# Expert stage of a graph and mixture-of-experts layer: second layer and results three tiles behind the first layer instead of two

## What is computed

```python
x = x + gnn(layernorm(x), edges, W, b)        # agg[dst] = x[src]; [x, agg] @ W.T + b
t = layernorm(x)
p = softmax(t @ router_w.T); rw, re = top_k(p, 2); rw = rw / rw.sum()
out = t
for e in range(8):
    h = gelu(t @ w1[e] + b1[e])               # 256 -> 256
    out = out + combine[:, e] * (h @ w2[e] + b2[e])
x = x + out
```

## Time and profile before

| | |
|---|---|
| timed runs | 1039.62 us (1039.11 to 1040.34) |
| span of the profiled execution | 1216.1 us; no other time of it is given |
| PE, DVE, ACT, POOL busy over the span | 77%, 67%, 47%, 38% |
| expert stage in the span | about 748 to 1211 us |
| L928 | 3000 matmuls |
| L943 and L938 | 1500 and 250 matmuls |
| granted TensorE clock over the span | 0.868 of full |

### The profile page before, as it was taken

One profiled execution on the slowest core, in us unless ns is written; L12 is line 12 of the kernel. 1 busy time (PEld: TensorE's weight loads), 2 busy tenths in 40 slices (PEclk: granted clock), 3 DMA queues, 4 the chain that ended last, 5 costly groups with the idle time before them and its releaser, 6 DMA issues.

```text
span 1216.1 us, 28747 instructions
## 1 busy us (share of the span) xinstructions
PE 932.3 (77%) x9598; PEld 821.3 (68%) x9599; DVE 820.3 (67%) x1801; ACT 569.5 (47%) x1565; POOL 467.2 (38%) x529
## 2 busy tenths in 40 slices
PE   0488888888377888247659945999888889999987
PEld 0477777777266677137648924888677778878876
DVE  6999999998255555534637594776565666667656
ACT  1355555554144444034435523555454555555544
POOL 8000000001544445555455002555555555555553
PEclk9799999999698889655555557999999999999999
DMA  6920000001344433335345361222222222222220
GB/s 202 323 100 26 26 26 26 26 17 43 99 129 132 126 112 112 87 107 170 116 135 168 105 7 36 63 73 71 58 62 58 62 64 71 74 70 71 70 58 13
DMA packets 78990, 103.26 MB, mean 85 GB/s; under 512 B 22505, under 2 KB 64482, under 8 KB 78938
## 3 DMA queue, kind: packets, MB, share of 16 engines
q0 software_dynamic: 21408, 54.87, 16.0%
q1 hardware_dynamic: 57530, 47.73, 13.9%
HBM read 62.12 MB, written 44.02 MB: 87 GB/s over the span
## 4 chain that ended last, share of the span: by engine, by line
PE 43%; DVE 21%; another core or an unknown queue 13%; issue 12%; ACT 8%; ACTq 1%; DMA 1%; DVEq 0%; POOL 0%; POOLq 0%
PE bank L928 10%; PE bank L943 9%; DVE arena L1040 7%; PE bank L748 5%; DVE arena L1027 5%; PE bank L771 5%; PE bank L829 4%; PE bank L894 3%; PE bank L840 2%; ACT arena L720 2%; PE bank L938 2%; ACT arena L682 1%; PE bank L792 1%; ACT arena L589 1%
## 5 line engine op out<-in xcount | busy, mean ns | idle before, releaser
L492 POOL DMA_INDIRECT arena<-key_rows,cid x98 | 93.9, 959 | 370.7 <-DVEq L1135 272.3
L928 PE MATMUL bank<-arena,w1s 128*128 128x128 f16 x3000 | 199.6, 221 | 28.9 <-issue 24.8
L928 PEld LDWEIGHTS bank<-arena,w1s 128*128 x3000 | 180.2, 99 | 43.2 <-issue 39.1
L943 PE MATMUL bank<-w2s,arena 128*128 x1500 | 199.8, 274 | 0.9 <-issue 0.8
L519 POOL DMA_INDIRECT out<-arena,gidx x125 | 128.8, 1030 | 177.7 <-DVE arena L1338 114.2
L508 POOL DMA_INDIRECT arena<-tok_rows,gidx x125 | 125.3, 1002 | 107.6 <-DVE gidx L1314 69.7
L771 PE MATMUL bank<-wgs,arena 128*128 128x256 f16 x1176 | 162.7, 295 | 0.0
L943 PEld LDWEIGHTS bank<-w2s,arena 128*128 128x128 f16 x1500 | 147.6, 98 | 18.0 <-issue 0.9
L707 ACT ACTIVATE arena<-bank 128x256 f16<-128x256 f32 x125 | 48.1, 385 | 222.9 <-remote 139.4
L771 PEld LDWEIGHTS bank<-wgs,arena 128*128 128x128 f16 x1176 | 124.4, 106 | 27.6
L720 ACT ACTIVATE arena<-bank,b1s 128x128 f32<-128x128 f32 x500 | 142.1, 374 | 1.2 <-PE bank L928 1.2
(11 more groups left out here) (215 smaller groups left out, 1515.0 us busy)
## 6 DMA issues: line engine op xcount, KB each, us to landing
agg_rows<-arena SPq DMA_DIRECT2D x49, 256.0 KB
tok_rows<-arena SPq DMA_DIRECT2D x13, 896.0 KB
big<-x SPq DMA_DIRECT2D x6, 1792.0 KB, 15.1
arena<-w SPq DMA_DIRECT2D x16, 256.0 KB, 2.9
arena<-tok_rows,gidx POOLq DMA_INDIRECT x125
out<-arena,gidx POOLq DMA_INDIRECT x125
big<-x SPq DMA_DIRECT2D x1, 1664.0 KB
arena<-key_rows,cid POOLq DMA_INDIRECT x98
```

The source lines that it names most:

```text
L492: gp.indirect_dma_start(er[:, b % 2, s, :], None, key_rows, bass.IndirectOffsetOnAxis(cid[:, t:t + 1], 0)).then_inc(er_full[b % 2], 16)
L928: last = mm(bank[2 + u % 2][:, at:at + P], parts[x, w, c, f], a[:, u % 4, c * P:(c + 1) * P], start=(n == 0), stop=(n == 5))
L943: last = mm(to, a[:, u % 4, at:at + P], parts[x, w, c], start=False, stop=(n == 5))
```

## The change

PE's second layer and DVE's result are taken three tiles behind the first layer instead of two, and the last written-out steps are one more. The place of each in its engine's step stays as it was, and so do all the other distances (tokens two ahead, hidden layer one behind), the buffers and POOL's order.

```diff
+BEHIND = 3
@@ schedule
-            for j in range(last * DEPTH, NT + 2):
+            for j in range(last * DEPTH, NT + BEHIND):
@@ pe_step
-                if j is None or 0 <= j - 2 < NT:
-                    tile_out(*tile(i, u, -2), second_layer(experts_of(known, (u if j is None else j) - 2)))
+                if j is None or 0 <= j - BEHIND < NT:
+                    tile_out(*tile(i, u, -BEHIND), second_layer(experts_of(known, (u if j is None else j) - BEHIND)))
@@ dve_step
-                if j is None or 0 <= j - 2 < NT:
-                    result(*tile(i, u, -2))
+                if j is None or 0 <= j - BEHIND < NT:
+                    result(*tile(i, u, -BEHIND))
```

## The result

The changed kernel takes 1049.57 us (median of four runs, 1048.62 to 1050.37) where the kernel before takes 1039.36 beside it: a ratio of 1.0092, with an interval of 1.0076 to 1.0108. It is slower by about 10 us, and the prediction of 1039.5 with its range up to 1048 missed it. The execution profiled has a time of its own of 1050.37 us over a span of 1048.3.

A forecast was written before the change was run, and what follows sets the result against it. PE's own work was taken to bound the expert stage, 3.10 us a step, 388 of its 463 us. The terms 0 + 0 + 0 - 0.1 = -0.1 us took 1039.62 to 1039.5 us, with a range of 1030 to 1048.

The forecast's parts named there:

- The late signal: ACT's L707 starts 1.73 us late behind PE's transposes in dense stretches of the trace; taken as absent from timed runs.
- Part (a): PE's order, second layer one step later: worth between 0 and 11.6 us of waits for L1325, taken as 0.
- Part (b): DVE's order and the hidden layer's buffers, results taken one tile later: zero, covered by the extra step.
- Part (d): Both ends of the expert stage: from -0.3 to +0.2 us, taken as -0.1.
- Part (c): POOL's store and gather issues move one step back, the change's only price: 0, with the gather's slack falling from 3.8 us.
- the slack of 0.7 us: Gather with a prompt signal: rows there at H + 9.96, wanted at H + 10.64, H being the first-layer burst's start.
- The gather becomes late: Rival: gathered rows land after PE's transposes want them, holding PE up; 1047 us, bounds 1043 and 1059, chance 0.21.
- 2 x 1.0 less 1.6: Late-gather price per trip of eight: about 1.0 us added twice, some 1.6 of L1325 waits gone; given as 27.7 from 27.45.
- no change: Likeliest case: no change that can be told, part sum -0.1 us, own range 1038 to 1041, chance 0.52.
- The low half did hold PE up: Rival: PE's second layer loses 5.6 to 11.6 us waiting for DVE's L1325, which the change frees; 1031.5 us, chance 0.27.
- a matmul record's hidden tail: PE's matmul records: their end is only an estimate and semaphore passing lies outside, so waits for L1325 could be in timed runs.
- waits of L894 for the gather's DMA: Sign in the changed kernel's trace: PE's transposes should now and then wait for gathered rows.
- The last sign: Timed runs moving by over 2 us either way would make the prediction wrong, with the late signal in them.

The follow-up runs named there:

- e1: The kernel before, unchanged, run and profiled again: 1040.42 us.
- e5 to e8: On a chip where the kernel before took 1215.23 us: gather ahead of store at two and four behind, sixteen slots at three and two behind; 1263.19, 1254.92, 1233.1, 1226.99 us.
- e11: The changed kernel with 16 slots for gathered rows instead of 8: 1037.34 us, ratio 0.9970.
- e13: The changed kernel with 16 slots for gathered rows and second layer and results four tiles behind: 1036.6 us, ratio 0.9969.
- e2: The changed kernel with POOL issuing the gather ahead of the store: 1041.07 us, ratio 1.0016.
- e3: The kernel before, distance still two, with only the gather issued one step later: 1050.01 us, ratio 1.0096.
- e14: The changed kernel with second layer and results four tiles behind, 8 slots, and the gather issued ahead of the store: 1093.33 us, ratio 1.0512.
- e4: The changed kernel with second layer and results four tiles behind instead of three, nothing else: 1214.04 us, ratio 1.1689.
- e12: The kernel before with 16 slots for gathered rows instead of 8: 1042.28 us, ratio 1.0021.
- e10: The kernel before with PE's transposes also waiting for the first expert's output added to an earlier tile (L1335): 1069.2 us, ratio 1.0274.

## Why the prediction was wrong

**The readings that held.** The late signal was taken to be in no ordinary timed run, and it is in none (e1), though it is a condition of some chip and not of the recording (e5 to e8). Part (a) was put at 0, on the ground that with a prompt signal the second layer has 1.2 us to spare: e1 has a single wait of 0.2 us for L1325, and with it gone the kernel gained nothing. Part (b), DVE's order and the buffers, costs little or nothing: e11 and e13 run at three and four behind without a loss. e2's 0.16% over the kernel before sits at the ends of the trips, whose last step is longer by 0.66 us instead of 0.53 (14 x 0.13 = 1.8); why, was not followed up. Part (d) was within half a us of nothing, too small to be seen beside the rest. Part (c) named the gather's later issue as the only price of the change, and it is (e3 has all of it, e2 almost none).

**The step that failed** is the sum of part (c), the slack of 0.7 us. Its first terms hold: the result ends 4.91 us behind the burst's start (4.90 in the sum), the gather starts at 7.08 (7.06), and half of the gathers land within 2.8 us. Two terms were mis-sized. The first is the end of the sum, the time at which the rows are wanted. It was put at 1.34, the start of the transposes. PE's sequencer comes to them at 0.43 to 0.47 and stops if the rows are not there, and the second layer is late when it gets past them after 1.09 or, in three steps of eight, after 0.67. Three steps on, less the gather's start, that leaves a gather 9.27 + 1.09 - 7.08 = 3.28 us, or 2.86, where the sum had 10.64 - 7.06 = 3.58.

The second is the landing time, one value for all. 2.90 and 2.85 were the first two gathers of the stage; over the changed kernel's stage the median is 2.8, but one in five takes more than 3.3 us, one in ten more than 3.6, and the longest 4.0 (4.8 in e1). The two together are the loss, and neither alone: a gather of the median 2.8 us is in time in every step, and had rows been wanted only when the array wants them, the spread would have cost little: the transposes themselves are late in nine of 116 tiles, 2.6 us in all. The sequencer stops in 66 tiles. Most of these lose nothing; in 23 the second layer is late by more than 0.05 us, 8.3 us in sum, and that is the loss of the stage to within 1.2 us. In the kernel before, with one step more, even a gather of 4.8 us is in time.

The rows of the kernel before at hand could have shown the first term: the register instructions of PE's sequencer are in the trace with their times. I read PE's and the weight loads' rows alone and took the row of the array for the time at which a semaphore is needed.

The dose follows the same sum. A result is finished in the step that is `distance` behind its tile's, and the rows gathered behind it are wanted six steps after the tile's own, so that the slack is (6 - distance) x 3.09 + w - 2.9, less the gather's start in its step (for the late gather of e3, one step fewer). With w = 0.45 it is the slack until the sequencer stops; with the mean of the two limits over a trip (0.99 for two behind, 0.93 for three, 0.88 for four, where four steps are of the second kind) it is the slack until the second layer is late:

| | gather starts | slack to a stop, us | slack to a loss, us | measured loss, us |
|---|---|---|---|---|
| two behind (before) | 7.13 | +2.8 | +3.3 | 0 |
| three, gather first (e2) | 5.18 | +1.6 | +2.1 | 1 to 2 |
| three (after), two with a late gather (e3) | 7.08, 7.11 | -0.3 | +0.2 | 10 |
| four, gather first (e14) | 5.23 | -1.5 | -1.1 | 53 |
| four (e4) | 7.1 | -3.4 | -2.9 | 174 |
| three or four, sixteen slots (e11, e13) | 7.7 | over 20 | over 20 | -3 |

Where the slack to a loss is negative, the ring of eight slots sets the pace, and two steps must last as long as the way round it. With the sequencer's 0.45 that is 4.8 a step for four behind and 3.8 with the gather first; with the limit of the loss it is (7.1 + 2.9 - 0.88) / 2 = 4.6 and (5.23 + 2.9 - 0.88) / 2 = 3.6, against 4.58 and 3.59 measured. For e4 the agreement is looser than it looks: 7.1 is the undisturbed start, and in e4 late transposes push the results back as well, so that the gather starts at 8.2.

**The rivals.** *The gather becomes late* was the right mechanism, priced at 1047 with bounds of 1043 and 1059, and came out at 1049.6. But it was given its chance of 0.21 for a wrong reason: it was said to decide by the late signal, and the point from which it decides was the sum with 1.34 in it. It decided with the prompt signal, by a path that the rival did not name: mostly not the transposes waiting for the rows, but the instructions behind them. Its price holds a slip too: 2 x 1.0 less 1.6 is 0.4 a trip, 27.85 and not 27.7, +6 us and not +4. A slack of 0.7 us, with a landing time read from two gathers, was no ground for 0.52 on no change. *The low half did hold PE up* was wrong here, and showed itself only with trips of sixteen (e12). The lower end of the range was wasted on it.

Of the pages of the Trainium skill, one is measured otherwise. For the waits for L1325 the prediction drew on what the Trainium skill says of a matmul record's hidden tail; e1 bounds that tail at 0.03 us, between L894's modelled end and L707's start. In the table of the same section (Perfetto Trace Analysis, Tensor Engine Instruction) an instruction is pushed into a wait queue, and the sequencer is then ready for the next while the semaphore wait goes on in the queue. Here the sequencer does not get past the transposes, whose first weight load has the wait: the next register instruction comes 0.04 us behind the landing in 66 of 116 tiles, and 0.05 behind the semaphore in steps 1 to 5 and 7 of e10's trips. The measurement decides. The other page of the Trainium skill, DMA: Bandwidth & Descriptors, section Anatomy of one DMA — SWDGE (gpsimd) path, states 2.0 us plus bytes/436,000; its estimate of 2.3 us would have made the slack larger still; the traces have 2.8 in the median.

**The profile's signs.** The prediction's list had the sign right that appeared ("waits of L894 for the gather's DMA"), but it expected the rest of the loss there too. By the view of waits these are 1.0 us more than in before on PE's row and 1.9 on the weight loads'; what is larger is named "issue" at the instruction behind. The last sign said that a move by over 2 us either way would mean that the late signal was in the timed runs. They moved by 10, and it was not.

## What to carry to other kernels

For what PE waits for, take the due time from its sequencer, not from the instruction's own row. The register instructions around it show when the sequencer gets there (0.8 us earlier here), and the time from there to the next work on the array shows how late it may be before something is lost (0.2 or 0.6 us before the array's own time here). Idle time marked "issue" behind an instruction that waits on a semaphore can be that wait's price, and so can idle time that carries another engine's name; compare the time of the update that was really needed. A step of distance between producer and consumer is also a step off every ring of buffers whose place the consumer frees: before taking it, work out that ring's slack with the slowest tenth of its transfers, and if it is small beside their spread, deepen the ring first. Here the distance with eight slots cost 10 us. With sixteen slots it was worth 5 us against the kernel before with sixteen, and 3 against the kernel before.

## What the runs showed of the hardware that was not expected

- PE's sequencer does not get past the transposes while their semaphore is not there: 0.04 us from landing to its next instruction in 66 of 116 tiles. A wait that is met before the array needs it can still cost: in steps 5 to 7 of e10's trips the transposes load at their usual 1.29, and the second layer is 0.11 to 0.17 us late.
- An indirect gather of 128 rows of 1040 bytes takes 2.8 us from its start to its landing in the median, over 3.3 in one case of four or five, and up to 4.8 (e1).
- On one chip the kernel before took 1215 us instead of 1040, at a granted clock of 0.87 instead of 0.90, and in such an execution ACT sees PE's transposes 1.7 us late in dense stretches, against 0.03 elsewhere (e1).
- The step that ends a trip of the hand-written loop is 0.5 to 0.7 us longer on PE, whether the trip has 8 or 16 steps, with the sequencer's last register instruction 0.1 us ahead of the burst (e1).
